# Loading a stack's k rows from ScalarE's queue, and another order of the opening units, in an attention block on one core

## The reference

```
x = L0_attn_X                                  # (2, 1024, 256), float32
x = layernorm(x + attention(x))
x = layernorm(x + ffn(x))

attention: Xn = layernorm(X) * ln_g + ln_b
  Q, K, V = split_heads(Xn @ Wq + bq), ..., ... # 16 heads of 16
  scores = Q @ K^T / sqrt(16), causal           # -inf above the diagonal
  A = softmax(scores);  out = (A @ V) @ Wo + bo
ffn: h = relu(x @ W1 + b1);  alpha = softmax(h @ W2 + b2)   # 8 experts
  out = sum_k alpha_k * U_k @ (V_k @ x)         # rank 64
```

## Time and profile before

| | us |
|---|---|
| median of 3 runs | 431.72 (431.71 to 434.21) |
| profiled execution | 431.88 |
| its span, first to last instruction | 429.9 |
| PE busy | 405.0 (94%) |
| DVE busy | 307.0 (71%) |
| ACT busy | 243.3 (57%) |
| POOL busy | 78.5 (18%) |

### The profile page before, as it was taken

How to read it: one execution, slowest core, us unless ns; L and a number is a source line. 1 busy time by engine, 2 the same in 40 slices (tenths; PEclk the granted TensorE clock), 3 DMA queues, 4 the chain that set the end, 5 groups by cost and what they waited for, 6 DMA issues and landing times.

```text
span 429.9 us, 7414 instructions
## 1 busy us (share of the span) xinstructions
PE 405.0 (94%) x2565; PEld 213.7 (50%) x2565; DVE 307.0 (71%) x807; ACT 243.3 (57%) x541; POOL 78.5 (18%) x115
## 2 busy tenths in 40 slices
PE   7997899999999989999999999999999998999994
PEld 3545444344334444476668734344334444446783
DVE  5548997798798676438488799789889863213665
ACT  6646555666777576443451264667676847642421
POOL 4422211143250110102240022113212011020000
PEclk9999999999999999999999999999999999999998
DMA  6167860450402000002673045054130000000011
GB/s 196 23 97 101 196 97 10 74 76 8 72 19 82 2 2 0 2 1 74 106 130 59 26 79 91 7 84 70 20 57 3 0 3 1 2 0 2 0 50 49
DMA packets 18452, 21.14 MB, mean 49 GB/s; under 512 B 4976, under 2 KB 11888, under 8 KB 18416
## 3 DMA queue, kind: packets, MB, share of 16 engines
q1 hardware_dynamic: 18365, 20.66, 25.7%
q10 hardware_dynamic: 51, 0.01, 0.0%
HBM read 5.79 MB, written 2.10 MB: 18 GB/s over the span
## 4 chain that ended last, share of the span: by engine, by line
PE 76%; DVE 15%; ACT 6%; issue 2%; DMA 1%; POOL 0%; ACTq 0%; DVEq 0%; POOLq 0%
PE ps L953 19%; PE ps L1068 14%; PE ps L1047 14%; PE ps L1024 10%; DVE mx L824 8%; PE ps L961 8%; PE ps L969 4%; PE ps L944 2%; ACT pr L683 2%; PE ps L1028 2%; PE ps L1142 2%; PE ps L1078 1%; DVE ps L820 1%; ACT stk L604 1%; DMA stq<-mrow 1%
## 5 line engine op out<-in xcount | busy, mean ns | idle before, releaser
L683 ACT ACTIVATE pr<-ps 128x512 f32<-128x512 f32 (+3 forms) x384 | 165.9, 495 | 95.3 <-PE ps L1047 93.8
L824 DVE TENSOR_REDUCE mx<-ps 128x1 f32<-128x512 f32 (+3 forms) x240 | 145.7, 665 | 14.6 <-PE ps L1024 7.4
L1047 PE MATMUL ps<-stq,stk 99*128 99x512 bf16 (+3 forms) x384 | 116.2, 330 | 4.8 <-ACT pr L683 3.3
L1024 PE MATMUL ps<-stk,stq 96*128 96x512 bf16 (+3 forms) x384 | 112.5, 327 | 1.4 <-DVE mx L824 0.6
L595 POOL TENSOR_SCALAR_AFFINE_SELECT pr<-pr 128x512 f32<-128x512 f32 x64 | 40.9, 639 | 245.9 <-ACT pr L683 245.9
L1068 PE MATMUL ps<-pr,va 128*32 128x512 f32 (+3 forms) x768 | 81.8, 498 | 0.0
L1047 PEld LDWEIGHTS ps<-stq,stk 99*128 99x128 bf16 x384 | 34.4, 98 | 90.8 <-ACT pr L683 51.8
L1024 PEld LDWEIGHTS ps<-stk,stq 96*128 96x128 bf16 x384 | 37.5, 98 | 21.4 <-issue 5.6
L820 DVE CUSTOM_DVE_ANT_0 ps<-ps,causal 128x384 f32<-128x384 f32 (+1 forms) x64 | 38.5, 648 | 11.6 <-PE ps L1024 11.6
L1028 PE MATMUL ps<-mask,ident_b 128*128 128x128 bf16 x192 | 35.2, 219 | 0.0
L953 PE MATMUL ps<-u_t,avt 128*128 128x256 f32 x128 | 30.8, 383 | 0.3 <-ACT avt L719 0.2
(11 more groups left out here) (108 smaller groups left out, 389.1 us busy)
## 6 DMA issues: line engine op xcount, KB each, us to landing
stq<-qk_raw SPq DMA_DIRECT2D x32, 96.0 KB, 2.8
stk<-qk_raw SPq DMA_DIRECT2D x32, 96.0 KB, 2.8
x_in<-in_x SPq DMA_DIRECT2D x8, 256.0 KB, 3.5
stq<-qk_raw SPq DMA_DIRECT2D x32, 64.0 KB, 2.4
stk<-qk_raw SPq DMA_DIRECT2D x32, 64.0 KB, 2.4
out_y<-x SPq DMA_DIRECT2D x3, 512.0 KB, 3.1
stk<-qk_raw SPq DMA_DIRECT2D x32, 32.0 KB, 2.4
stq<-qk_raw SPq DMA_DIRECT2D x32, 32.0 KB, 2.1
```

The costliest lines, as they stand in the source:

```text
L683: nc.scalar.activation(probs(b, g, s)[:, j, q0 - c * CHUNK:], act_bank(ev)[:, q0 - c * CHUNK:], ACT.Exp, scale=DH ** -0.5).then_inc(s_act_ ...
L824: nc.vector.tensor_reduce(dst, src, AX.X, ALU.max).then_inc(s_dve_free, 1)
L1024: last = nc.tensor.matmul(bank[:, i * w:(i + 1) * w], q[0:ROWS, t // TPC, j, tile(t % TPC)], k[0:ROWS, k0 // CHUNK, j, 0:w], start=True, s ...
L1047: nc.tensor.matmul(bank[:, q0 - c * CHUNK:], stk[stack_of(b, g)][0:ROWS + PARTS, kt // TPC, j, tile(kt % TPC)], stq[stack_of(b, g)][0:ROWS ...
```

## The change

Two things are changed.

First, of the stack of the second group, first chunk, first sequence, the six DMAs to k rows are no longer issued by SP but by ScalarE. ScalarE issues one of them behind each of six of its events: values of tiles 0 and 2, the first projection of chunk 1 for q, and the middle parts of three projections. Each waits for the high, middle and low parts of chunk 0.

Second, the opening is in another order. Two units stand ahead of the third projection of chunk 1 (before, one), one unit between it and the last projection (before, three), and the other two near units behind the last projection. At the end of the opening, two units of the second group move ahead of the values of tile 6 and of the rows of the first group's maxima.

```diff
         if b == 0:
             at_split = opening.index(("split", 0, 0, 0))
             near = sum(ev[0] == "max" and max_units(tiles)[ev[3]][3][-1] < HPG // 2 for ev in opening[:at_split])
-            order += qks[:2] + woven(qks[2:-1], opening[:near]) + qks[-1:]
-            order += woven(opening[near:at_split], vs[0][2:3]) + [opening[at_split]] + vs[0][3:] + opening[at_split + 1:]
+            order += qks[:2] + opening[:2] + qks[2:3] + opening[2:3] + qks[3:] + opening[3:near]
+            rows, *rest_of_opening = opening[at_split + 1:]
+            order += woven(opening[near:at_split], vs[0][2:3]) + [opening[at_split]] + rest_of_opening[:2] + vs[0][3:] + [rows] + rest_of_opening[2:]
...
                             sp.dma_start(q[q_rows, c, heads], same).then_inc(s_stack[stack_of(b, g)][c][i], 16)
-                            sp.dma_start(k[k_rows, c, heads], k_parts[:, 0:part_of_q + 1]).then_inc(s_stack[stack_of(b, g)][c][i], 16)
+                            if (b, g, c) != (0, 1, 0):
+                                sp.dma_start(k[k_rows, c, heads], k_parts[:, 0:part_of_q + 1]).then_inc(s_stack[stack_of(b, g)][c][i], 16)
...
+            loads = [(i, row, n) for i in range(2) for row, n in ((5 * DH, 1), (3 * DH, 2), (0, 3))]
+            behind = [("v", 0, 0), ("v", 0, 2), ("qk", 0, 0, 1, 0), ("part", 0, 0, 1, 0), ("part", 0, 0, 1, 1), ("part", 0, 1, 1, 0)]
...
+                if ev in behind:
+                    i, row, n = loads[behind.index(ev)]
+                    k_parts = parts(1, 0)[(2 + i) * DH:(3 + i) * DH].rearrange("p n m s -> p n (m s)")
+                    act.wait_ge(s_high, n_high["qk", 0, KC - 1, 0, 1])
+                    act.wait_ge(s_mid, n_part["part", 0, KC - 1, 0, 1])
+                    act.wait_ge(s_low, n_part["part", 0, KC - 1, 0, 1])
+                    act.dma_start(stk[1][row:row + n * DH, 0, 2 * i:2 * i + 2], k_parts[:, 0:n]).then_inc(s_stack[1][0][i], 16)
```

## The result

The changed kernel took a median of 433.46 us (431.89 to 435.14, 19 runs), the kernel before 431.77 us beside it (431.55 to 434.21, 19 runs). The ratio is 1.0042 [1.0033, 1.0051]: 0.4% slower, where 0.1% faster was forecast. That is inside the range and within 1%, but on the wrong side of no change, and clear of it.

A forecast was written before the change was run, and what follows sets the result against it. TensorE, busy 405.0 of 429.9 us, was taken as the bound, and the change's worth as how far the first score matmul moves. Terms -0.3 + 0 - 0.1 + 0 = -0.4 us gave 431.3 us, range 430.5 to 434.0.

The forecast's parts named there:

- The front of the opening: TensorE's opening order: last projection ends 1.16 us sooner, leaving 0.3 us at the DMA of the first maxima's rows.
- Six issues on ScalarE at nothing: ScalarE's six k-row issues, taken at 0.9 us each, hide in its free time: cost 0, up to +2.6 us.
- The rival of slow issues: Each of ScalarE's six issues takes 1.2 to 1.5 us, giving 432.5 to 434.3 us; chance 0.17.
- the one long issue: ScalarE's only earlier DMA issue, 1.51 us; by the skill's rule, its own time plus one of SP's.
- This alone is worth 0: SP loses six issues, 3.8 us with gaps; no TensorE wait before names those loads, so worth 0.
- rows' DMA: First maxima's rows, no longer first DMA on ScalarE's queue: -0.1 us, bounds -0.6 and 0.
- The likeliest case: The forecast itself, 430.7 to 431.9 us for the whole kernel, unmoved loads included; chance 0.52.
- TensorE's clock falls: Rival: TensorE idles 2.9 us before the first score and its clock drops, +1 to +2.5 us; chance 0.20.
- the sum: Terms for opening order, ScalarE's issues, the maxima rows' DMA and k rows' landing, together -0.4 us.
- VectorE's stall: VectorE's 0.90 us wait before the second group's first maximum goes, returning as some 2 us at its seventh.
- The gain that carries: Rival: VectorE's 0.90 us and the projection's 1.16 us stay in hand, about -1.1 us, 430.6; chance 0.08.
- the stated range: Whole kernel, 8 in 10: 430.5 to 434.0 us, taking in the gain, the clock's price and most slow issues.

The follow-up runs named there:

- experiment 7: Changed kernel with the end of the opening as before, keeping the order around the two projections and ScalarE's k-row loads: 430.96 us, ratio 0.9973.
- experiment 8: Kernel before with only the order of units and projections at the opening's front changed, SP still loading the k rows: 430.81 us, ratio 0.9973.
- experiment 2: Changed kernel with SP's five weight loads held back until the first rows of maxima have landed: 432.50 us, ratio 1.0012.
- experiment 1: Changed kernel with 13 spare matmuls on TensorE directly ahead of the wait for the first rows of maxima: 431.83 us, ratio 1.0008.
- experiment 9: Changed kernel with the opening's end as before and SP's weight loads held until the first rows have landed: 430.84 us, ratio 0.9966.
- experiment 4: Changed kernel's order, with the second group's k rows loaded by SP again: 434.33 us, ratio 1.0057.
- experiment 10: Kernel before with the rows of the first maxima moved ahead of the values of tile 6: 435.12 us, ratio 1.0059.
- experiment 6: Changed kernel with the rows of the first maxima ahead of tile 6's values, still behind the second group's two units: 431.18 us, ratio 0.9977.

## Why the prediction was wrong

*The front of the opening* held. The last projection was put at 27.83 and stood at 27.71 net of the start. That little of it reaches the DMA, since the values of tile 6 stand behind two more units, held too: 0.3 us forecast, 0.19 measured. Experiments 7 and 8 show the other side of that step, which was not carried further: without the two units 0.62 to 0.65 us of it reach the rows, and the median is 0.9 to 1.1 us under the kernel before.

*Six issues on ScalarE at nothing* held, and at 0.54 to 0.67 us each they cost less than the 0.9 taken. The rival of slow issues falls. So does the reading that the prediction made of the one long issue by the Trainium skill, Perfetto Trace Analysis, section "DMA Instruction — HWDGE", as waiting for the lock of a shared block: in experiment 2 SP issued nothing from 38.41 on, 0.16 us after the rows' issue had begun, and the issue still took 1.33 us on ScalarE, against 1.34 with SP issuing back to back. What makes this shape dearer on ScalarE than the 0.89 us of the earlier trace rows stays open.

*"This alone is worth 0", of SP's six issues,* failed. Nothing on TensorE named those loads, which was true and not enough: what a queue does when it is done sooner counts as well. The weight loads moved up to 0.23 us behind the rows' DMA, and the term "rows' DMA", forecast at -0.1 us, measured +0.94 in the profiled execution (4.18 us from issue to score, 3.24 before). On the medians, holding the loads back takes 1.0 us off (experiment 2), 0.9 of it among executions with a fallen clock.

*The likeliest case* failed, and it decides the sign. That TensorE's clock falls was named as a rival, at its right place and with about its right price (+1 to +2.5 us; experiment 1 takes 1.6 off), and given 0.20. The row that bore on it was read as a doubt: the clock had held over 1.39 us and was lost some 2.4 us after the last matmuls, and the forecast's own numbers put the new wait at 2.9. That is past the longer row, and in the trace of after it was 3.72. It should have been the likeliest case. Also, the sum was made of a path of waits whose durations were taken as fixed, though the wait changes the durations behind it: the clock stood in it at nothing and measured 1.84 us. In the profiled execution, net of its start, the sum of -0.4 us came out as -0.19 at the issue, +0.94 at the DMA and +1.84 of clock, 2.6 us in all.

*VectorE's stall* went and came back at the seventh maximum, as forecast, but at 3.32 us in place of some 2. *The gain that carries* came near (430.81 and 430.96 for 430.6) only in the kernels that keep the end of before.

That the time lies inside the stated range is owed to the clock's price, which the range took in, and not to the sum.

The medians lay the loss out: 433.46 for the kernel after, 431.83 with spare matmuls (1.6 less), 432.50 with the loads held (1.0 less), 431.29 with both (2.2 less). The two do not add up to their sum, and held loads alone also make falls of the clock rarer (8 of 12 for 18 of 19). With the end of before it is 430.96, 0.3 us less than with both cures; the intervals of these two overlap, so a price of the two moved units by themselves is not shown.

What stays open: what in the weight loads stretches the rows' DMA (in experiment 1, with nearly the same distance between the issues, it took 3.0 us at most), why it took 2.35 to 3.10 us in the traces where the loads were far from it or held, and why the clock falls in one execution and not in the next of the same kernel. None of these kernels was tried with spare matmuls in what is left of the wait in experiment 8.

## What to carry to other kernels

When a change lengthens a wait of TensorE, even beside a gain elsewhere, compare the new wait with the longest over which the trace shows the clock held, and price the work behind it at half clock if it is longer, for as long as the traces show a fall to last (here 3.4 or 6.8 us). A shorter wait is not safe for that, as experiment 9 shows. Spare matmuls in the wait cost nothing that could be measured here while they ended before the DMA landed. When a queue gets shorter, look at what it issues next, and beside which small, awaited DMA it will fall. And measure the parts of a change by themselves: here the first line of the order is worth 1 us, ScalarE's queue alone nothing that can be told, and with the second line added the kernel loses more than that gain, with that queue (433.46) and without it (434.33).

## What the runs showed of the hardware

- The clock's fall outlasts its cause, and lasted one of two lengths. Where it came inside the wait it was 6.8 us at 1.2 GHz (42.7 to 49.5 in the kernel after, 40.4 to 47.3 in experiment 2). Where it came when TensorE was back at work it was 3.4 us (experiments 4, 9 and 10: from 43.1, 41.2 and 37.9, which is 0.8, 0.4 and 0.1 us after the wait's end).
- It comes by execution. By their mean clocks it was 18 of 19 of the kernel after (wait 3.72 us in its trace), 8 of 12 in experiment 2 (2.15), at least 13 of 85 of the kernel before (1.39).
- ScalarE's DMA issue runs beside the ACTIVATE ahead of it, yet holds up the one behind it: no gap between the ACTIVATEs around the issue at 30.55 in the kernel after, 1.41 us in experiment 6.
- Loads of weights issued 0.23 us behind the DMA of 48 rows: 4.18 us from issue to score; 0.34 us behind: at most 3.1; 1.2 us or more behind, or held: 2.5 to 3.2 (3.24 in the kernel before, 3.19 in experiment 9 with the loads held).
